# Graph attention over eight sequences on one core: projection steps, release lags and prologue order rearranged

## The reference

```python
h = maximum(layernorm(x), 0)                 # x: 8 sequences x 1024 tokens x 512
q, k, v = (heads(h @ W + b) for q, k, v)     # 16 heads of 32
scores = einsum('bhqd,bhkd->bhqk', q, k) / sqrt(32)
scores = where(adj[:, None] == 0, -inf, scores)
out = softmax(scores) @ v                    # per head, then heads side by side
return x + out @ Wo + bo
```

## Time and profile before

| | us |
|---|---|
| median of three runs | 1907.11 |
| the runs | 1906.05 to 1907.27 |
| the profiled execution | 1910.52 |
| its span (first to last instruction) | 1908.4 |
| TensorE busy | 1852.2 (97%) |
| VectorE busy | 1544.2 (81%) |
| ScalarE busy | 1482.4 (78%) |
| GpSimd busy | 1584.4 (83%) |
| mean granted TensorE clock | 0.995 |

### The profile page before, as it was taken

How to read it: one execution, slowest core, us unless ns; L and a number is a source line. 1 busy time by engine, 2 the same in 40 slices (tenths; PEclk the granted TensorE clock), 3 DMA queues, 4 the chain that set the end, 5 groups by cost and what they waited for, 6 DMA issues and landing times.

```text
span 1908.4 us, 35624 instructions
## 1 busy us (share of the span) xinstructions
PE 1852.2 (97%) x13856; PEld 772.6 (40%) x13856; DVE 1544.2 (81%) x1585; ACT 1482.4 (78%) x1772; POOL 1584.4 (83%) x701
## 2 busy tenths in 40 slices
PE   6989999999999999999999999999999999999987
PEld 3334434444344443444444434344444444344332
DVE  6778877888878887788877888778877888777875
ACT  4968896788967888678886888768887688967763
POOL 0988989788997989978998888978889789898864
PEclk9999999999999999999999999999999999999999
DMA  7423342423524335233442325433353334433211
GB/s 242 141 72 92 115 133 90 132 77 111 158 71 129 89 113 152 74 109 97 134 121 91 107 80 147 119 100 106 93 135 112 108 92 122 126 97 92 59 39 46
DMA packets 167772, 206.16 MB, mean 108 GB/s; under 512 B 18864, under 2 KB 117296, under 8 KB 167600
## 3 DMA queue, kind: packets, MB, share of 16 engines
q1 hardware_dynamic: 166736, 203.50, 36.3%
q10 hardware_dynamic: 864, 0.34, 0.1%
HBM read 153.43 MB, written 50.33 MB: 107 GB/s over the span
## 4 chain that ended last, share of the span: by engine, by line
PE 78%; DVE 9%; ACT 5%; issue 4%; POOL 3%; DMA 0%; DVEq 0%; SPq 0%; POOLq 0%; ACTq 0%
PE ps L772 21%; PE ps L759 20%; PE ps L727 14%; PE ps L741 8%; PE ps L809 7%; DVE ring L1057 7%; PE ps L734 6%; POOL acc L1274 3%; ACT ring L894 3%; PE ps L782 1%; PE ps L723 1%; DVE hT_lo L1066 0%; ACT squares L918 0%; DMA ring<-x 0%; PE ps L737 0%
## 5 line engine op out<-in xcount | busy, mean ns | idle before, releaser
L1057 DVE TENSOR_TENSOR ring<-ps,mask 128x1024 f32<-128x1024 f32 x1024 | 1220.7, 1218 | 295.3 <-PE ps L759 248.3
L894 ACT ACTIVATE ring<-ring 128x1024 f32<-128x1024 f32 x1024 | 1066.8, 1052 | 301.6 <-DVE ring L1057 288.1
L1274 POOL TENSOR_TENSOR acc<-acc,ring 128x1024 f32<-128x1024 f32 x380 | 910.5, 2424 | 25.9 <-ACT ring L894 25.7
L1274 POOL TENSOR_TENSOR acc<-ring 128x1024 f32<-128x1024 f32 x252 | 599.4, 2400 | 256.8 <-ACT ring L894 256.6
L759 PE MATMUL ps<-q_stack,k_stack 128*128 128x512 f16 x2048 | 604.0, 382 | 26.9 <-DVE ring L1057 23.0
L772 PE MATMUL ps<-ring,v_sb 128*32 128x512 f32 x4096 | 507.6, 602 | 0.1
L759 PEld LDWEIGHTS ps<-q_stack,k_stack 128*128 128x128 f16 x2048 | 162.7, 98 | 380.6 <-DVE ring L1057 141.0
L772 PEld LDWEIGHTS ps<-ring,v_sb 128*32 128x32 f32 x4096 | 107.5, 109 | 264.2 <-issue 214.7
L809 PE MATMUL ps<-acc,ones 128*32 128x512 f32 x1008 | 131.2, 592 | 0.0
L734 PE MATMUL ps<-wv_hi,hT_lo 128*128 128x128 f16 x1024 | 100.1, 219 | 0.0
L734 PE MATMUL ps<-wv_hi,hT_hi 128*128 128x128 f16 x1024 | 100.1, 219 | 0.0
(11 more groups left out here) (88 smaller groups left out, 1518.3 us busy)
## 6 DMA issues: line engine op xcount, KB each, us to landing
x_in<-x SPq DMA_DIRECT2D x172, 256.0 KB, 3.0
edges<-adjT SPq DMA_DIRECT2D x128, 256.0 KB, 3.2
q_stack<-q_parts SPq DMA_DIRECT2D x256, 128.0 KB, 3.0
k_stack<-k_parts SPq DMA_DIRECT2D x256, 128.0 KB, 3.1
q_parts<-q_part SPq DMA_DIRECT2D x128, 128.0 KB, 1.9
k_parts<-k_part SPq DMA_DIRECT2D x128, 128.0 KB, 2.3
out<-x_in SPq DMA_DIRECT2D x60, 256.0 KB, 2.0
ring<-x SPq DMA_DIRECT2D x4, 512.0 KB, 5.5
```

Of the source, the lines that this page charges most:

```text
L894: nc.scalar.activation(tile, tile, ACT.Exp, scale=SCALE / UP / UP).then_inc(s["prob_ready"], 1)
L1057: nc.vector.tensor_tensor(ring[:, slot_of(kt, pair), :].rearrange("p (a n) -> p a n", n=HALF), ps_s(j), mask[:, kt:kt + 1, half * HALF:(ha ...
L1274: nc.gpsimd.tensor_tensor(acc[:, group, pair, :], first_of, ring[:, slot_of(kt, pair), :], ALU.add).then_inc(s["sum_done"], 1)
```

## The change

It touches tables and five places of code. `PRODUCTS`, `HIGH_AFTER`, `SQUARE_AFTER`, `LOW_AFTER` and the tables of statistics, normalisation, bias and mask get other steps; no chunk is added or removed. The low part of Wo is made in four quarters at steps 5, 8, 11 and 14. The last unit gets its own steps for the output's high and low part (5, as before, and 7 instead of 9). In the prologue, the second q no longer waits for the first k's high part; the first two thirds of the first v come between the first and the second part of the second q, its last third behind the second k, ahead of the first scores; DVE makes two low parts of h ahead of the first k's. The second v stays in step 0, behind the norms.

```diff
 PRODUCTS = [
-    {("q", 0): (0, 2), ("q", 1): (2, 5), ("k", 0): (5, 8), ("y", 0): (8, 9), ("k", 1): (10, 13), ("y", 1): (16, 16), ("v", 0): (17, 21), ("y", 2): (22, 22), ("y", 3): (22, 24), ("y", 4): (26, 29), ("v", 1): (29, 32), ("n", 0): (32, 32)},
-    {("q", 0): (1, 4), ("y", 5): (5, 6), ("y", 6): (7, 10), ("q", 1): (10, 13), ("y", 7): (16, 17), ("k", 0): (18, 21), ("v", 0): (21, 23), ("k", 1): (25, 26), ("v", 1): (28, 31), ("n", 0): (31, 32)},
-    {..., ("t", 0): (13, 13), ("q", 1): (14, 18), ("t", 1): (19, 19), ("k", 1): (20, 23), ("v", 1): (25, 28), ("t", 2): (28, 29), ("t", 3): (29, 30), ("n", 0): (31, 31), ("t", 4): (32, 32)},
-    {("t", 5): (1, 1), ("q", 0): (2, 5), ("k", 0): (7, 8), ..., ("q", 1): (15, 19), ("k", 1): (20, 20), ("v", 1): (23, 28), ("n", 0): (28, 28)},
+    {("q", 0): (0, 2), ("q", 1): (2, 5), ("k", 0): (5, 6), ("y", 0): (6, 9), ("k", 1): (10, 15), ("y", 1): (16, 16), ("v", 0): (17, 21), ("y", 2): (22, 22), ("y", 3): (23, 24), ("y", 4): (24, 29), ("v", 1): (29, 32), ("n", 0): (32, 32)},
+    {("q", 0): (1, 4), ("q", 1): (5, 7), ("y", 5): (8, 10), ("y", 6): (11, 13), ("y", 7): (16, 17), ("k", 0): (18, 21), ("v", 0): (21, 23), ("k", 1): (24, 25), ("n", 0): (27, 28), ("v", 1): (28, 31)},
+    {..., ("t", 0): (13, 15), ("q", 1): (16, 18), ("t", 1): (19, 19), ("k", 1): (20, 23), ("v", 1): (25, 28), ("t", 2): (28, 29), ("t", 3): (29, 29), ("n", 0): (30, 31), ("t", 4): (32, 32)},
+    {("t", 5): (1, 1), ("q", 0): (4, 6), ("k", 0): (7, 8), ..., ("q", 1): (15, 19), ("k", 1): (20, 22), ("v", 1): (24, 28), ("n", 0): (28, 28)},
 ]
 HIGH_AFTER = [
-    {("q", 0): 0, ("q", 1): 0, ("k", 0): 0, ("k", 1): 1, ("v", 0): 1, ("v", 1): 0},
+    {("q", 0): 0, ("q", 1): 0, ("k", 0): 0, ("k", 1): 1, ("v", 0): 2, ("v", 1): 0},
...
 LOW_AFTER = [
-    {("q", 0): 1, ("q", 1): 2, ("k", 0): 2, ("k", 1): 2, ("y", 0): 2, ...},
+    {("q", 0): 2, ("q", 1): 1, ("k", 0): 1, ("k", 1): 2, ("y", 0): 2, ...},
...
-    {("q", 0): 1, ("t", 5): 4, ("k", 0): 4, ("t", 6): 1, ("t", 7): 1, ("q", 1): 2, ("k", 1): 2, ("n", 0): 1},
+    {("q", 0): 2, ("t", 5): 5, ("k", 0): 3, ("t", 6): 1, ("t", 7): 2, ("q", 1): 3, ("k", 1): 1, ("n", 0): 1},
 ]
-MASK_AT = {3: [18, 19, 20, 23, 26, 27, 29, 30], 0: [1, 5, 6, 9, 11, 12, 14, 18]}
+MASK_AT = {3: [16, 17, 19, 24, 25, 26, 28, 29], 0: [1, 5, 7, 9, 13, 14, 18, 21]}
-O_HIGH_AT, O_LOW_AT = [4, 15, 10, 5], [7, 19, 13, 9]
+O_HIGH_AT, O_LOW_AT = [4, 16, 10, 5], [6, 18, 13, 9]
+OUT_WEIGHTS_AT = (5, 8, 11, 14)
+LAST_O_HIGH_AT, LAST_O_LOW_AT = 5, 7
-EARLY_LOWS = [("t", 0), ("t", 1), ("t", 2), ("t", 3), ("q", 0), ("k", 0), ("t", 4), ("t", 5), ("t", 6), ("t", 7), ("q", 1), ("k", 1)]
+EARLY_LOWS = [("t", 0), ("t", 1), ("t", 2), ("t", 3), ("q", 0), ("t", 4), ("t", 5), ("k", 0), ("t", 6), ("t", 7), ("q", 1), ("k", 1)]
...
                         if first and up == 0 and j == 0:
-                            early("v", 0)
                             early("n", 0)
                             early("v", 1)
...
                 if kind in "qk":
-                    pe.wait_ge(s["w_hi_ready"], "qk".index(kind) + 1)
-                    pe.wait_ge(s["high_ready"], QT // 2 * (t + 1) + (2 if t else 0))
-                    products(kind, t, 0, 0, DC, bank, None)
+                    early_rounded(kind, t)          # waits for high_ready of QT // 2 * (t + 1) alone
+                    if (kind, t) == ("q", 1):
+                        early_v_rounded()           # 32 of the 48 products: high and low h times high weights
...
             for kind, t in PRO_CHUNKS[:QT + 4]:
                 early(kind, t)
+            early_v_low()                           # the other 16: high h times low weights
             pe.wait_ge(s["const_loaded"], 16 * 2)
             scores(0, 0, 0)
...
-                        if first and up == 1 and j == 7:
-                            weights_low(3)
+                        if first and up == 1 and j in OUT_WEIGHTS_AT:
+                            out_weights_low(OUT_WEIGHTS_AT.index(j))
...
-                        if j == O_LOW_AT[up] and not (first and up == 0):
+                        if j == (LAST_O_LOW_AT if last and up == UNITS - 1 else O_LOW_AT[up]) and not (first and up == 0):
                             o_low(U - 1, (up - 1) % UNITS)
```

More of the change, by code:

```diff
@@ L868, in early, with early_rounded, early_v, early_v_rounded @@
                     products(kind, t, 0, 0, PIECES[kind], bank, x_first(t) if kind == "t" else None).then_inc(s["chunk_ready"], 1)
+            def early_rounded(kind, t):
+                pe.wait_ge(s["w_hi_ready"], "qk".index(kind) + 1)
+                pe.wait_ge(s["high_ready"], QT // 2 * (t + 1))
+                products(kind, t, 0, 0, DC, early_bank(PRO_CHUNKS.index((kind, t))), None)
+            def early_v(parts_of_v):
+                bank = early_bank(PRO_CHUNKS.index(("v", 0)))
+                for tt in range(QT // 2):
+                    for n, (hl, wl) in enumerate(parts_of_v):
+                        for c in range(DC):
+                            i = nc.tensor.matmul(bank[:, tt * P:(tt + 1) * P], (hT_hi, hT_lo)[hl][:, c, tt * P:(tt + 1) * P], (w_hi, w_lo)[wl][WV][:, c, 0:P],
+                                                 start=(tt, hl, wl, c) == (0, 0, 0, 0), stop=(tt, wl, c) == (QT // 2 - 1, 1, DC - 1))
+                return i
+            def early_v_rounded():
+                pe.wait_ge(s["low_ready"], LOWS_BEFORE[BANK_LEFT_BY["v", 0]])
+                pe.wait_ge(s["w_hi_ready"], 3)
+                early_v(((0, 0), (1, 0)))
+            def early_v_low():
+                pe.wait_ge(s["w_lo_ready"], 3)
+                early_v(((0, 1),)).then_inc(s["chunk_ready"], 1)
             pe.wait_ge(s["ident_loaded"], 16)
@@ L972, in graph @@
                             o_high_last(0)
-                        if j == O_HIGH_AT[up] and not (first and up == 0):
+                        if j == (LAST_O_HIGH_AT if last and up == UNITS - 1 else O_HIGH_AT[up]) and not (first and up == 0):
                             y_read = chunk_no(ALL, (b, 1, "y", QT - 1)) + 1 if up == 1 and not first else None
@@ L1209, in weights_low, with out_weights_low @@
                     .then_inc(s["w_lo_ready"], 1)
+            def out_weights_low(c):
+                dve.wait_ge(s["w_hi_ready"], 4)
+                i = nc.vector.scalar_tensor_tensor(out=w_lo[WO][:, c, :], in0=staging(WO)[:, c, :], scalar=UP, in1=w_hi[WO][:, c, :],
+                                                   op0=ALU.mult, op1=ALU.subtract)
+                if c == DC - 1:
+                    i.then_inc(s["w_lo_ready"], 1)
             def normalise_first(t):
@@ L1235, in _ @@
             dve.wait_ge(s["const_ready"], 5)
-            early_low("q", 0)
-            early_low("k", 0)
-            for t in range(QT // 2, QT):
-                early_low("t", t)
+            for kind, t in EARLY_LOWS[QT // 2:QT + 2]:
+                early_low(kind, t)
             weights_low(2)
```

8 lines of the change are left out of this document (4 added, 4 removed), and 20 rows, old and new, of tables (HIGH_AFTER, LOW_AFTER, PRODUCTS, SQUARE_AFTER).

## The result

The changed kernel takes 1916.4 us (median of five runs, 1909.4 to 1917.2) against 1907.1 before: 1.0033 times as long, 95% interval 1.0020 to 1.0047. (That ratio is the one on record; the quotient of the two medians is 1.0049, so the loss is somewhere between 4 and 9 us.) I had predicted 1894.9, faster, and gave slower a chance of 0.06. The profiled execution after took 1916.72 us with a span of 1914.6, the one before 1910.52 with 1908.4, so the two traces differ by 6.2 us; the rest of the 9.3 is that the execution before lay 3.4 above its median.

What follows compares the result with a forecast made beforehand. PE was taken as the bound, 97% busy, with idle time mainly at the ends. Terms -2.7 + 0.6 - 4.6 - 1.7 - 3.8 = -12.2 us from the median 1907.1 gave 1894.9, range 1889.5 to 1903.

Steps and rivals of the forecast that it cites:

- The repeating sequences: Units between the ends: waits of 2.6 instead of 2.9 us, -0.25 a sequence, -1.7 over seven stretches; bounds -9 and +5.
- the rule for PE's waits: Any stretch of steps: DVE's 2.03 us plus 1.13 per further tile plus other pieces' own time; excess over PE's work is wait.
- the one on exact hand-overs: Rival: unit 0, step 17, ACT late with k's high part, so PE loses time seven times; slower, e.g. 1912; chance 0.05.
- Unit 1 of the first sequence: Quartering Wo's low part and moving chunks cuts lost time from 8.0 to 3.4 us: -4.6; bounds -6 and -2.5.
- quarters of 0.82 (a fourth of 3.28) instead of 0.67: First sequence, unit 1: price in us of each quarter of Wo's low part; at 0.82 the term is -4.3, not -4.6.
- Prologue: Start of kernel: first scores stay at about 34.1, tile 2's come 2.7 us earlier: -2.7; bounds -3.0 and -0.5.
- The last unit: Low part of o at step 7 instead of 9: PE resumes 2.8 us sooner, keeps its clock: -3.8; bounds -4.3 and -1.
- real end: Last unit: POOL's maximum over partitions may really end at 1860.84, so DVE's step 20 verdict waits, giving part back.
- Unit 0: First sequence: +1.6 at steps 9 and 10, -0.65 at step 17, -0.4 at steps 4 and 5: +0.6; bounds 0 and +1.5.
- The second: Rival that the ends give half: clock falls before first scores, quarters contend, POOL holds last unit; -4.7, 1902.4 us; chance 0.17.
- The fourth: Rival: repeating sequences lose 1 to 1.7 us each from low parts waiting for ACT; about 1906, no change; chance 0.06.
- The signs that I had named: Wrong if: step 17 waits in unit 0, sequence above 231.5, first scores after 35 or half clock, last verdict waiting for POOL.

Runs made afterwards that it cites:

- the first cured kernel: Kernel after, with POOL waiting for unit 2's low part of o, Wo's low part whole at step 4, last-unit bias addition waiting for limit operations: 1892.6 us.
- the run with the old order of low parts: The first cured kernel, with the first k's low part again ahead of the fifth and sixth of h on DVE in the prologue: 1892.7 us (two runs).
- the kernel before with the three cures: Kernel before, with last unit's low part of o at step 7, POOL's wait for its limit operations, Wo's low part at step 4: 1902.7 us, ratio 0.9958.

## Why the prediction was wrong, point by point

**The repeating sequences** (-0.25 each, bounds -9 and +5 together; measured +8.75 in the trace, with the other stretches between the ends). With the exclusion out of the way the term is -0.3, but that it fits is in part luck: the waits as I printed them add up to 2.8 and 2.7, not 2.9 and 2.6, and give -0.1. What failed is the step "the rule for PE's waits", which gives each DVE piece "its own time". The low part of o takes 1.28 or 3.46 us, by whether it starts 0.2 us before or 0.01 us after an addition of POOL's. I had asked what the moved chunks do to PE, DVE and ACT, and never what an earlier exponential does to the start of POOL's next addition. That is 1.6 us in each of six sequences (the fifth had it before) and 0.6 in the eighth. None of my rivals had it: the one on exact hand-overs looked at step 17 of unit 0, and PE did not wait there.

**Unit 1 of the first sequence** (-4.6, measured +2.0; +3.2 against the 61.2 to 61.4 that the old tables took in three other profiled executions). The failed step is the price of a quarter, "quarters of 0.82 (a fourth of 3.28) instead of 0.67". I read the two durations, 3.28 and 2.28, as the same work done slower beside POOL. They are the same work after a wait: in every trace with the whole instruction beside POOL it ends 2.15 us after the addition in which it started, and the difference is what was left of that addition. A wait does not divide by four. Each of the four pieces can meet an addition of 2.38 us, so its upper bound was about 0.6 + 2.4 = 3.0, and the first came close with 2.85. With 12 us for four as the bound, where one piece took 3.28, the split itself would have been the rival that ends on the other side. The 0.82 that I gave as the price "by the page" is a fourth of 3.28; the page has no price. The sentence that I cited (GPSIMD Engine Reference of the Trainium skill, section Specifications) says that the two contend; another page of it, SBUF — State Buffer, section "SBUF: two separate sides", says what I missed: the pair of ports is an exclusive lock, the one that starts first has it for its whole instruction, and the other is fully blocked. The traces agree for these instructions: 2.37 + 1.08 = 3.45 against 3.46 measured. The addition that began inside a memset and still came second is the one observation that this leaves open.

What the moved chunks did there was right in direction: with Wo in one piece the unit took 60.74, 0.5 to 1.8 less than with the old tables.

**Prologue** (-2.7, bounds -3.0 and -0.5; measured -2.8 alone; in the change 0.0 to the end of unit 0, so -0.5 after unit 0's own cost). Alone, the size was right within its interval; in the profiled execution of the change the bound "-0.5" is what came. I had named its cause, the clock, and that the second q's stores might be issued under the k loads; what I had not seen is that the q loads before them take 0.8 to 1.5 us longer to issue.

**The last unit** (-3.8, measured -4.5 in the change, -7.5 alone). The direction and the first half, the low part of o and PE's clock behind it, were right, worth 3.0 up to tile 20 in both runs. That the total came near -3.8 in the change is luck: the rest lies at step 20, and the same code gave 4.2 more in two other executions. I had looked for POOL at step 20 and bounded the gain by its "real end", but not seen that the two limit operations there were already paying 3.7 us for POOL's bias additions before.

**Unit 0** (+0.6) came as said: 54.12 us with the new tables (Wo in one piece) against 53.66 with the old ones (prologue alone), both at full clock, so +0.5.

**The rivals.** None of the four was the case as it stood. The second's conditions came (half clock over the first scores, quarters that contend), but it priced the quarters at +1.0, where this unit came out 6.6 above its term. The fourth had the size, 1.4 a sequence, and another cause: a low part late for ACT, where it was late for POOL; it also took all other terms as they stood, and so came to 1906. The signs that I had named did show: a repeating sequence above 231.5 (231.95), waits above 1.5 us in unit 1 of the first sequence, first scores at 34.8 and at half clock.

## What to carry to other kernels

Where DVE and POOL both work from SBUF, list the DVE instructions with two SBUF inputs, and the small ones, by their duration, shortest and longest. A 128x4 operation of 2.4 us and a form with two durations were waits for POOL here, and the timeline of POOL at its start shows which addition. Before such an instruction is split, count the additions that its pieces can meet, and make its order against POOL by a semaphore instead of leaving it to tenths of a us; a wait on POOL, where POOL has idle time, cost nothing here and gave 14 us. And a change that only moves work has to be followed to the start of every engine's next instruction, also of the engine it doesn't touch.

## What the hardware showed that I had not expected

- One engine blocks, it is not slowed: the low part of o ends 1.08 us after POOL's addition whenever it starts in one (seen for rests of 0.28 to 2.38 us; where only 0.1 of the addition is left it takes its usual 1.28), a quarter of Wo's 0.55 and the whole of Wo's 2.15 after. An operation on 128x8 elements with two SBUF inputs (`shift`) took 2.01 us in the kernel before, in seven sequences, where it starts in an addition, and 0.16 after, where it doesn't. Mask subtractions and low parts that read PSUM, and a reduction, ran beside POOL at their usual times.
- Behind a 128x256 memset in float32, POOL's addition, issued 0.1 us after the memset's start, came second to the DVE instruction that followed it. Why is not shown.
- PE's clock went by more than the last wait. Behind a wait of 2.14 us the first scores ran at full clock (Wo in one piece), behind one of 2.17 at a mean of 0.58 (after); 2.34, 2.48 and 2.52 were each followed by windows at 0.72 to 0.74, and so were, in the first cured kernel, two waits of only 0.99 and 1.12 with little work around them. The same code can go either way: these two waits left the clock at 1.00 in the run with the old order of low parts; the wait for h's low parts in the old prologue was followed by 0.53 in the kernel before (2.06 us) and by 1.00 in the kernel before with the three cures (2.07 us). So my reading that a wait of 2.06 costs the clock and one of 0.99 does not was drawn from too few rows. What decides it is not shown.
- Runs of one kernel differ by up to 17 us (1896 to 1913 for the one with POOL's wait in unit 2). The profiled executions differ in the clock over the first scores and in the limit operations of the last unit; that these explain the whole spread was not shown.
